# Expert tiles of a mixture-of-experts layer: outputs a tile later and ahead of the first layer, residual and store a turn later, 39 tiles

## What is computed

```python
logits = xr @ moe_gate_w + moe_gate_b              # xr: 4096 tokens x 256
top_v, top_i = jax.lax.top_k(logits, 2)
chosen = jnp.max(top_i, axis=-1)                   # one expert of 8 for each token
def expert(W1, B1, G, Bt, W2, B2, rsc):            # W1 256 x 512, W2 512 x 256
    hh = xr @ W1 + B1
    hh = jax.nn.gelu(_ln(hh, G, Bt), approximate=False)
    return (hh @ W2 + B2) * rsc + xr
sel = outs[chosen]                                 # the chosen expert's row
```

## Time and profile before

| | us |
|---|---|
| median of 3 runs | 2434.81 |
| lowest and highest run | 2431.68, 2436.64 |
| span of the profiled execution | 2427.9 |
| expert tiles, first x transpose to last finish | 1474.8 to 1676.3 |
| PE busy, DVE busy over the span | 1834.8, 1503.7 |

### The profile page before, as it was taken

One profiled execution on the slowest core, in us unless ns is written; L12 is line 12 of the kernel. 1 busy time (PEld: TensorE's weight loads), 2 busy tenths in 40 slices (PEclk: granted clock), 3 DMA queues, 4 the chain that ended last, 5 costly groups with the idle time before them and its releaser, 6 DMA issues. The chain is left out here.

```text
span 2427.9 us, 30628 instructions
## 1 busy us (share of the span) xinstructions
PE 1834.8 (76%) x8414; PEld 842.9 (35%) x8415; DVE 1503.7 (62%) x2941; ACT 974.9 (40%) x1285; POOL 604.2 (25%) x581
## 2 busy tenths in 40 slices
PE   4799794999999999999987816995068974018885
PEld 2355461222222222222215613553034541015443
DVE  5688345887887887888823424554677975871111
ACT  1455361366565665666663302332224542001110
POOL 3344245000000000000003443334543431082332
PEclk8999896799999999999998858998589987558998
DMA  4000385112211111211003051111200014002332
GB/s 117 0 0 0 106 285 175 32 32 48 48 32 33 32 32 33 50 44 32 1 15 138 0 186 55 56 56 57 74 0 0 0 47 144 0 11 61 101 93 30
DMA packets 112375, 137.11 MB, mean 56 GB/s; under 512 B 14209, under 2 KB 88449, under 8 KB 112001
## 3 DMA queue, kind: packets, MB, share of 16 engines
q1 hardware_dynamic: 97280, 113.59, 15.8%
q0 software_dynamic: 9216, 16.79, 3.0%
q10 hardware_dynamic: 5760, 5.25, 0.6%
HBM read 78.44 MB, written 57.15 MB: 56 GB/s over the span
## 5 line engine op out<-in xcount | busy, mean ns | idle before, releaser
L873 DVE TENSOR_REDUCE sa_mpart<-sa_a 128x1 f32<-128x512 f32 x1024 | 653.6, 685 | 143.0 <-PE sa_a L959 136.2
L941 ACT ACTIVATE sa_e<-sa_b 128x1024 f32<-128x1024 f32 x512 | 499.4, 1022 | 315.2 <-PE sa_b L986 315.0
L959 PE MATMUL sa_a<-sa_k,sa_q 96*128 96x512 bf16 x1024 | 386.6, 404 | 61.0 <-DMA sa_k<-k_parts 26.6
L986 PE MATMUL sa_b<-sa_q,sa_k 98*128 98x512 bf16 x1024 | 311.2, 387 | 9.4 <-issue 7.0
L996 PE MATMUL sa_ops<-sa_e,sa_v 128*17 128x512 f32 x2048 | 273.0, 604 | 0.0
L959 PEld LDWEIGHTS sa_a<-sa_k,sa_q 96*128 96x128 bf16 x1024 | 87.5, 98 | 452.4 <-DVE sa_mpart L873 406.6
L1098 POOL TENSOR_TENSOR ao_var<-ao_mv,x_eps_pow 128x4 f32<-128x4 f32 x8 | 1.6, 201 | 908.6 <-DVE ao_mv L1197 908.6
L300 POOL TENSOR_TENSOR xa_prob<-xa_prob,xa_rden 128x1024 f32<-128x1024 f32 x64 | 121.6, 1902 | 189.8 <-DVE xa_rden L247 189.8
L421 PE MATMUL xa_score<-xa_kblk,xa_qst 128*128 (+1 forms) x256 | 132.4, 622 | 20.3 <-ACT xa_qst L343 19.2
L986 PEld LDWEIGHTS sa_b<-sa_q,sa_k 98*128 98x128 bf16 x1024 | 97.1, 99 | 107.3 <-issue 38.8
L2320 PE MATMUL sw_p<-sw_xT,tc_w 128*128 128x512 f32 x256 | 114.1, 604 | 1.2 <-ACT sw_xT L2342 1.2
(11 more groups left out here) (306 smaller groups left out, 2706.2 us busy)
## 6 DMA issues: line engine op xcount, KB each, us to landing
sa_q<-q_parts SPq DMA_DIRECT2D x16, 768.0 KB, 6.3
sa_k<-k_parts SPq DMA_DIRECT2D x16, 768.0 KB, 9.2
tc_w<-in_L_ffn_W SPq DMA_DIRECT2D x24, 512.0 KB, 4.7
k_parts<-sp_kpart SPq DMA_DIRECT2D x16, 384.0 KB, 3.1
q_parts<-sp_qpart SPq DMA_DIRECT2D x16, 384.0 KB, 2.9
expert_in<-ao_zero SPq DMA_DIRECT2D x1, 5120.0 KB, 22.8
expert_out<-ex_xb ACTq DMA_DIRECT2D x40, 128.0 KB, 1.7
v_groups<-sp_vt SPq DMA_DIRECT2D x8, 544.0 KB, 3.6
```

Source lines behind the costliest of these rows:

```text
L873: nc.vector.tensor_reduce(mpart[par][:, head, rest // 2, rest % 2:rest % 2 + 1], aps[k % 2][:], axis=X, op=ALU.max).then_inc(max_done, 1)
L941: nc.scalar.activation(ex[kt % 2][p][:], bps[p][:], ACT.Exp, scale=SCALE).then_inc(exp_done, 1)
L959: nc.tensor.matmul(aps[k % 2][:], qs[s][0:KROWS, head, q0:q0 + P], ks[s][0:KROWS, head, (rest % 2) * CW:(rest % 2 + 1) * CW], start=True, ...
L986: last = nc.tensor.matmul(bps[p][:, head % 2], ks[s][:, head, kt * P:(kt + 1) * P], qs[s][:, head, qc * CW:(qc + 1) * CW], start=True, sto ...
```

## The change

MT becomes 39 (with at least one token, eight experts can't leave more than seven extra tiles over 32). 39 is no multiple of four, so `turns` runs one group of four, a loop over eight groups, and the last three turns singly. PE's outputs become a function of their own; turn k is now: x transposes of k+3, h transposes of k, outputs of k-1, first layer of k+3. DVE's finish is done for k-2 rather than k-1, still behind add_b1 and ahead of apply_norm. ACT's store is done for k-3 and comes first in the turn. POOL's rstd comes ahead of add_b2. The semaphore values that each function waits for are the same.

```diff
--- before.py
+++ after.py
@@ -1035,7 +1035,7 @@
                 transpose_out(UNITS)
 
 E8 = 8
-MT = TILES + E8
+MT = TILES + E8 - 1
 F1 = 512
 FK = F1 // P
 
@@ -1434,11 +1434,11 @@
 
             for j in range(U):
                 body(j, 0, j, True)
-            with eng.Fori(1, MT // U - 1) as i:
+            with eng.Fori(1, MT // U) as i:
                 for j in range(U):
                     body(i * U + j, i, j, True)
-            for j in range(U):
-                body(MT - U + j, MT // U - 1, j, j + AHEAD < U)
+            for k in range(MT // U * U, MT):
+                body(k, k // U, k % U, False)
 
         def expert(eng, k):
             return eng.value_load(tile_expert[0:1, ds(k, 1)], min_val=0, max_val=E8 - 1)
@@ -1461,7 +1461,7 @@
                     load(k, k)
                 turns(sp, body)
                 for i in range(U):
-                    sp.wait_ge(y_stored[i], 16 * (MT // U))
+                    sp.wait_ge(y_stored[i], 16 * len(range(i, MT, U)))
 
             @block.tensor
             def _(pe):
@@ -1493,8 +1493,12 @@
                     for f in range(FK):
                         last = nc.tensor.transpose(tps[j % 2][:, f * P:(f + 1) * P], hb[j][:, f * P:(f + 1) * P], ident[:])
                     last.then_inc(hT_psum, 1)
+                    if later(k, 1):
+                        outputs(k - 1, (j - 1) % U)
                     if ahead:
                         hidden(k + AHEAD, (j + AHEAD) % U)
+
+                def outputs(k, j):
                     e = expert(pe, k)
                     pe.wait_ge(hT_ready, k + 1)
                     pe.wait_ge(y_ready, k + 1)
@@ -1508,6 +1512,7 @@
                     transpose_x(k, 0, k)
                     hidden(k, k)
                 turns(pe, body)
+                outputs(MT - 1, (MT - 1) % U)
 
             @block.scalar
             def _(act):
@@ -1534,17 +1539,17 @@
                     act.dma_start(gathered_out[ds(P * k, P), :], xb[j][:]).then_inc(y_stored[j], 16)
 
                 def body(k, turn, j, ahead):
+                    if later(k, 3):
+                        store(k - 3, (j - 3) % U)
                     if ahead:
                         evacuate_xT(k + AHEAD, (j + AHEAD) % U)
                     gelu(k, j)
-                    if later(k, 2):
-                        store(k - 2, (j - 2) % U)
 
                 for k in range(AHEAD):
                     evacuate_xT(k, k)
                 act.wait_ge(ew["b_loaded"], ew["b_count"])
                 turns(act, body)
-                for k in (MT - 2, MT - 1):
+                for k in range(MT - 3, MT):
                     store(k, k % U)
 
             @block.vector
@@ -1573,8 +1578,8 @@
                 def body(k, turn, j, ahead):
                     if ahead:
                         add_b1(k + AHEAD, (j + AHEAD) % U, expert(dve, k + AHEAD))
-                    if later(k, 1):
-                        finish(k - 1, (j - 1) % U)
+                    if later(k, 2):
+                        finish(k - 2, (j - 2) % U)
                     if ahead:
                         apply_norm(k + AHEAD, (j + AHEAD) % U)
 
@@ -1587,7 +1592,8 @@
                     add_b1(k, k, expert(dve, k))
                     apply_norm(k, k)
                 turns(dve, body)
-                finish(MT - 1, (MT - 1) % U)
+                for k in range(MT - 2, MT):
+                    finish(k, k % U)
 
             @block.gpsimd
             def _(pool):
@@ -1607,10 +1613,10 @@
                                             ALU.add).then_inc(xb_ready, 1)
 
                 def body(k, turn, j, ahead):
+                    if ahead:
+                        make_rstd(k + AHEAD, (j + AHEAD) % U)
                     if not isinstance(k, int) or k + 1 < MT:
                         add_b2(k + 1, turn + (j + 1) // U, (j + 1) % U)
-                    if ahead:
-                        make_rstd(k + AHEAD, (j + AHEAD) % U)
 
                 pool.wait_ge(ew["b2_scaled"], 1)
                 pool.wait_ge(y_ready, 2)
```

## The result

| | before | changed |
|---|---|---|
| median of 4 runs, us | 2433.28 | 2571.81 |
| lowest and highest run | 2431.68, 2436.64 | 2557.15, 2576.13 |
| span of the profiled execution | 2427.9 | 2571.9 |
| expert tiles, last finish starts at | 1675.86 | 1817.97 |

The account below looks back on a forecast made before the run. PE bounds the expert-tile stage at 4.77 us a tile; the change makes a DVE-PE wait chain of 7.06 us. Stage 66.7 us later plus 25.5 us of halved clock, added to 2434.8, gives 2527 us, range 2493 to 2560.

Parts of the forecast that it names:

- the stall: PE's outputs wait for DVE's finish behind add_b1: 7.06 us a turn against 4.77, 34 stalls, stage ending 66.7 us later.
- The unknown release from DVE to PE: DVE's semaphore to PE's next start, shown by no row: taken as 0.14 us, between 0.05 and 0.25.
- Rival 1: Expert-tile stage: the stall is there but the clock stays up, 2501.5 us; chance 0.27.
- the price of the clock: PE's clock in the expert-tile stage halves in every second turn, 17 x 1.5 = 25.5 us, bounds 0 and 58 us.
- such a rule: Skill's rule that bursts between waits are throttled every time; backed the rival of a clock fall every turn, 2559 us, chance 0.15.
- rows 9: Second cross-attention: bursts 6.83 us apart with 2.30 us gaps at clock 1.00, cited for the clock staying up.
- one edit costed at nothing: POOL's rstd ahead of add_b2, on which SP's load for x's transposes hangs: taken to cost nothing.
- the tail: End of the expert-tile stage gets quicker: last three outputs 2.33, 2.33 and 1.9 us apart, last finish starting at 1742.6.
- the missing tile: Expert-tile stage: the missing 40th tile is worth 4.77 us, already in the 66.7 us.
- the store at no cost: ACT's store ahead of the xT copy waits for finish, but xT is ready 0.96 us before the first layer.
- rival 4: ACT closes a longer chain through a late xT copy, 1 us a turn more, 2561 us; chance 0.04.
- Rival 3: The stall is covered, finish(k-3) running before add_b1(k+2) on DVE: a turn of 4.42 us, 2412 us; chance 0.03.

Follow-up runs that it names:

- experiment 3: Changed kernel with five matmuls more a turn on PE ahead of the outputs, results read by nobody: 2508.94 us, ratio 1.0300 to the kernel before.
- experiment 1: Changed kernel with DVE's finish alone undone, again of tile k-1: 2467.51 us, ratio 1.0132 to the kernel before.
- experiment 2: Changed kernel with finish of k-2 kept but put ahead of add_b1 on DVE: 2478.64 us, ratio 1.0166 to the kernel before.
- experiment 7: Changed kernel with the outputs behind the first layer again, finish still of k-2 and behind add_b1: 2585.67 us, ratio 1.0615 to the kernel before.
- experiment 6: Changed kernel with POOL's order alone undone, add_b2 ahead of rstd again: 2535.59 us, ratio 1.0404 to the kernel before.
- experiment 4: Kernel before with 39 tiles in place of 40 and the new layout of turns, all orders as before: 2428.64 us, ratio 0.9974.
- experiment 11: Kernel before with only the outputs' move and 39 tiles; finish, store and POOL as before: 2399.47 us, ratio 0.9863.
- experiment 5: Changed kernel with DVE's finish and POOL's order both undone: 2397.67 us, ratio 0.9841 to the kernel before.

## Why the prediction was wrong, step by step

**Right: the stall.** The chain through add_b1, moments, finish and outputs exists, and all 34 stalls are there; forecast 7.06 us a turn, measured without the clock's part 7.11 (experiment 3), 1.6 us more over the 33 turns. The unknown release from DVE to PE was 0.25, at the end of its bounds. The gap of 0.91 ahead of finish was DVE's own, as I had taken it: the trace now names no engine for it. Experiments 1 and 2 show that it is the finish's place that closes the loop, experiment 7 that the outputs' place does not. Rival 1, this stall with the clock up, was put at 2501.5; experiment 3 is near it, at 2508.9.

**Failed: the price of the clock.** The step was "I take a fall in every second turn ... a slow stretch of 3.4 us loses at most 1.7 us of the chain's PE work; part of it lies in the gap, so 1.5. 17 x 1.5 = 25.5 us. The bounds are 0 and 34 x 1.7 = 58 us." Measured: 33 turns took 300.0 us; at 7.11 each they would take 234.6; the clock's part is 65.4 us, above even the upper bound. Both factors were too small: 29 slow stretches instead of 17, at 2.3 us each (65.4 / 29) instead of 1.5. A slow stretch can last 6.4 us and more instead of 3.4 and then covers outputs and first layer both, 3.0 us lost (1.74 on the outputs, 1.22 on the first layer); and 21 of the 33 turns take 9.8 us or more, in a pattern of four turns, 10.06, 10.05, 9.81 and 7.63 us, that repeats from tile 11 on. I had one slow stretch in my rows and took its length for all. The Trainium skill, TensorE: Matmul & The Clock Gate, section "HAM oscillation — how this bites in real kernels", has it that bursts after long waits start throttled every time. Here three in four do (the outputs at 1601.43, 1611.56 and 1628.93), and in the fourth, at 1620.06, the clock falls while they run, so the page was nearer than my rows 9. Why the gaps of rows 9 left the clock up isn't shown. A reader who weighs such a rule against four undisturbed gaps should give the rule more than 0.15.

**Failed: one edit costed at nothing.** "SP's load hangs on add_b2 and feeds x's transposes, which stand ahead of the 2.5 us gap" holds for the stalled turns, but not for the first two, which have no gap. There the load was late: 9.43 us instead of 4.42, 5.0 us. Of these 3.5 are the wait, and 1.5 the half clock behind it (0.50 from 1498.47 to 1501.50). Experiment 6 has the turn at 4.43 with POOL's order undone.

**The account.** By the last finish of the two profiles, and without the 1.9 us that the stage started later, the miss is 142.1 - 1.9 - 92.2 = 48.0 us. Of it 5.0 are the load, 1.6 the chain, 65.4 - 25.5 = 39.9 the clock in the 33 turns, and 1.4 the tail, which took 15.4 us from tile 38's first layer to the last finish instead of 14.0, with the clock at half for parts of it (0.67 in the mean from 1808 to 1811 us). By the medians the miss is 138.5 - 92.2 = 46.3.

Other signs that the prediction named were missed with the clock: first layers 9.09 us apart, not 7.0 to 7.9; a granted clock of 0.76, not 0.8 to 0.9; PE busy for 70% of the stage's turns, not near 65% (it is busy for longer at the half clock); the stage's end 142 us later, not 60 to 120.

**Right:** the missing tile (experiment 4), the store at no cost (experiment 11 against 5), and the doubt about rival 4: ACT's copy never was the releaser. Rival 3, the covered stall, is what experiment 5 comes to, by another order on DVE; it lay at 2397.7 rather than 2412.

What stays open is what makes the clock fall behind one gap and not behind the next of the same length, and why the pattern of four turns settles in one run (the changed kernel's first trace) and only in places in another (experiments 6 and 8). A third pair of output buffers, which would also free the outputs from finish, was not tried. By the Trainium skill, Perfetto Trace Analysis, section "Optimization Strategy", equal bubbles that repeat can mean too little buffer space. These 33 do end with a buffer's release, but experiments 5 and 11 remove them with the buffers as they are, by the order alone.

## What to carry to other kernels

- When a step moves to a later turn, write down for each wait which turn of the other engine gives it and what stands ahead of it there. A wait with 1.5 us to spare became a loop of 7 us because the work that released it moved to a later turn, and there it stands behind work that waits for what the first engine has only just issued.
- Undo each part of a change by itself: the outputs' move was worth 1.2% in this kernel (2399.5 against 2428.6 with 39 tiles), hidden by two reorderings that came with it. The second, on POOL, cost about 3 us alone and 70 us once the first was mended.
- A repeated idle gap on PE can cost more than its length. Here 2.7 us of idling brought another 2 us a turn, and useless matmuls in the gap won back 42 to 63 us. The gaps of rows 9, 2.30 us, cost nothing of the kind, so it has to be measured.

## What was unexpected of the hardware

- Slow stretches of the clock came in two lengths, about 3 us (1611.2 to 1614.2) and over 6.4 us (1601.0 to 1607.4), and the lengthened turns then met the clock's changes again at the same places every four turns. As I read it, the loss kept itself up so; no run here shows that.
- With an idle gap in each turn, runs of one program lie further apart: 2520.03, 2528.04 and 2543.14 us in experiment 6, at a mean granted clock of 0.872, 0.869 and 0.862, where experiment 5's four stay within 4 us. The longer the run, the lower its clock.
- From DVE's end to PE's start it is 0.25 us (1611.31 to 1611.56), from ACT's 0.14.
